# First bias on TensorE, Gelu from PSUM and a joined residual in the quantised feed-forward stage of a two-layer decoder

## The chip, the cores and the metric

One core of one Trainium2 chip runs the whole program. The metric is the device time of one execution in microseconds (us).

## The reference

The program is two decoder layers on x of shape 8 x 256 x 512; each layer has attention, cross attention and a feed-forward part, each followed by a residual and a layer norm. The change lies in the last part, the quantised feed-forward network of the second layer:

```python
def activation_quant(x):
    scale = 127.0 / jnp.clip(jnp.max(jnp.abs(x), axis=-1, keepdims=True), EPS_Q)
    return jnp.clip(jnp.round(x * scale), -128, 127) / scale
def weight_quant(w):
    return jnp.sign(w) * jnp.mean(jnp.abs(w))
def bit_linear(x, w, b, dim_in):
    x_norm = simple_rms_norm(x, dim_in)
    x_q = activation_quant(x_norm)
    w_q = weight_quant(w)
    return jnp.einsum('bsd,od->bso', x_q, w_q) + b
h = bit_linear(x, w1, b1, DIM)          # 512 -> 2048
h = jax.nn.gelu(h, approximate=False)
return bit_linear(h, w2, b2, INNER)     # 2048 -> 512
x = _layernorm(x + ffn(x), axis=-1)
```

## The kernel before

The kernel is written engine by engine: each stage is one block with a program for each of the five engines, which meet only through semaphores. An engine runs its program strictly in the order written; whatever waits holds up all that stands behind it. The last stage is `quantised_ffn_stage`. x lies in SBUF as 16 tiles of 128 rows and 512 columns, two tiles (q = 0, 1) to each of the 8 blocks b. Whole numbers up to 127 and signs are held in bfloat16 and multiplied exactly; one scale per row turns the product back ("unit").

Before the rounds the stage loads the weights (`raw`, four pieces of 2 MB) and the biases, ScalarE squares all rows of x (L2255) and takes the signs of the weights (L2213), and VectorE sums their magnitudes (L2315) and works out the scales of x (L2297 to L2309, with three Newton steps of `inverse_root`, L50).

A block then passes through these steps:
- VectorE scales x (L2328), GpSimd bounds and rounds it (L2277, L2280), TensorE transposes it (L2127) and ScalarE copies it out of PSUM (L2206).
- First product: eight chunks of 512 columns, four bfloat16 matmuls each (L2143), into four PSUM banks. VectorE reads each chunk, multiplies by the unit, adds the first bias and writes it to SBUF (L2340); ScalarE takes the Gelu in place (L2222).
- VectorE takes the greatest value (L2352) while ScalarE squares and sums the rows (L2233); some seventeen small VectorE steps give the scales; VectorE scales h (L2356), ScalarE subtracts the rounding constant (L2248), VectorE clamps (L2375).
- TensorE transposes h in 32 pieces (L2127), ScalarE copies them out in four parts (L2203), and the second product takes 2 x 16 matmuls (L2159).
- VectorE multiplies by the unit and adds the second bias (L2363), adds the residual (L2368), and normalises the rows (L85 to L101) into x.

The rounds overlap two blocks: in `round_of(b)`, b from 0 to 8, "here" is block b up to its clamped rows, "prev" is the transposes, second product and layer norm of block b-1, and "next" the preparation of x for b+1. `has` (L152) leaves out what isn't there at the ends. Rounds 1 to 6 are a loop on each engine whose waits count up in registers; rounds 0, 7 and 8 are written out. PSUM for transposes has two banks, used in turn (`Turns`, L127); a transpose waits for the copy two turns back. `Steps` (L26) lets an engine wait for its own last small step.

## Time and profile before

| what | value |
|---|---|
| median of 3 runs | 2926.22 us (2924.99 to 2927.89) |
| the profiled execution | 2924.51 us |
| its span | 2922.7 us |
| busy share of the span | TensorE 85%, VectorE 62%, ScalarE 43%, GpSimd 10% |
| mean granted TensorE clock | 0.948 of full |
| last stage | from about 2630 us to the end |

Times are in us from the start of the span, PE is TensorE, PEld its weight loads, DVE VectorE, ACT ScalarE, POOL GpSimd. In a timeline, rows of one kind that follow each other are merged: "x16" is the number of instructions, and the bracket at the end is the idle time ahead of the first and what ended it. A line number is that of the kernel before. A granted clock of 1.0 is 2.4 GHz, of 0.5 1.2 GHz. In a chain of waits each piece is what the next one waited for, or the work ahead of it on its engine.

### The profile page before, as it was taken

Reading aid. Unit: us, or ns where it says so; the run is one execution under the profiler, and the core shown is the slowest. Engines: PE = TensorE matmul, PEld = TensorE weight load, DVE = VectorE, ACT = ScalarE, POOL = GpSimd, SP = SyncE. Lnnn points to the kernel's source line nnn. Section 1 sums busy time; section 2 is a strip of 40 time slices with the busy share of each in tenths; the row PEclk is TensorE's granted clock in tenths of the full one; section 3 lists DMA queues with packets and bytes.
Section 4 is the critical chain, followed back from the end, with each engine's and each line's share of the span. In section 5 each row is a group of like instructions: output and inputs, shape, how many; then the busy total and the mean of one; then the engine's idle time right before and its main releaser. Section 6 shows DMA issues by size and latency. Waiting matters only on the chain. (4 is left out here: it accounts for less than half of the span.)

```text
span 2922.7 us, 46388 instructions
## 1 busy us (share of the span) xinstructions
PE 2475.3 (85%) x15730; PEld 1911.1 (65%) x15746; DVE 1802.4 (62%) x5199; ACT 1264.8 (43%) x2994; POOL 297.9 (10%) x535
## 2 busy tenths in 40 slices
PE   5889999999983999799999999995888888874664
PEld 3668999999863999476677766763655555541332
DVE  5656767667775566445445544454666666657886
ACT  2334545444433222244444444452544444436563
POOL 3211001000000000000000000002111111102220
PEclk8999999999996999999999999997999999996887
DMA  4101211212005000000000000001000000003001
GB/s 155 59 24 36 77 33 37 69 39 75 30 1 217 0 0 0 2 1 0 0 1 0 0 1 0 0 1 51 5 4 4 4 4 4 4 1 133 0 0 58
DMA packets 41151, 82.45 MB, mean 28 GB/s; under 512 B 4528, under 2 KB 17840, under 8 KB 39856
## 3 DMA queue, kind: packets, MB, share of 16 engines
q1 hardware_dynamic: 41008, 80.70, 7.8%
q8 instruction: 70, 1.15, 0.2%
q14 instruction: 73, 0.60, 0.1%
HBM read 72.30 MB, written 8.39 MB: 28 GB/s over the span
## 5 line engine op out<-in xcount | busy, mean ns | idle before, releaser
L1990 DVE TENSOR_REDUCE s_nmax<-s_a_ps 128x2 f32<-128x512 f32 x256 | 174.2, 686 | 195.1 <-PE s_a_ps L1772 188.1
L647 ACT ACTIVATE s_p<-s_ms,s_nmax 128x256 f32<-128x256 f32 x256 | 128.5, 503 | 194.4 <-DVE s_nmax L755 194.4
L755 DVE CUSTOM_DVE_ANT_0 s_ms<-s_s_ps,s_bias 128x256 f32<-128x256 f32 x256 | 98.1, 421 | 179.5 <-PE s_s_ps L525 179.0
L1375 ACT ACTIVATE l_wo_w<-l_wo_w,s_nmax 128x128 f32<-128x128 f32 (+1 forms) x256 | 114.4, 447 | 199.2 <-DVE s_nmax L1471 198.4
L508 PE MATMUL s_q_ps<-s_xT,s_wh 128*128 128x256 f32 x1024 | 189.9, 286 | 0.0
L1215 PE MATMUL s_s_ps<-l_wqb_w,s_lT 128*128 128x512 f32 x384 | 175.9, 597 | 16.5 <-DVE l_wo_w L1441 15.8
L914 PE MATMUL s_h_ps<-s_xh,s_t 128*128 128x256 f32 x704 | 173.3, 285 | 9.4 <-DVE s_xl L1002 9.4
L1886 ACT ACTIVATE s_pT<-s_s_ps 128x512 f32<-128x512 f32 x256 | 151.6, 606 | 59.7 <-PE s_s_ps L1785 57.6
L558 PE MATMUL s_y_ps<-s_wh,s_oT 128*128 128x512 f32 x512 | 175.6, 404 | 0.0
L914 PE MATMUL s_h_ps<-s_xl,s_t 128*128 128x256 f32 x704 | 172.7, 284 | 0.0
L508 PEld LDWEIGHTS s_q_ps<-s_xT,s_wh 128*128 128x128 f32 x1024 | 165.7, 194 | 6.0 <-issue 0.5
L1772 PE MATMUL s_a_ps<-s_kTz,s_qTx 128*128 128x256 f32 x512 | 137.2, 351 | 33.3 <-DVE s_nmax L1990 31.8
L1471 DVE CUSTOM_DVE_ANT_0 l_wo_w<-s_s_ps,s_bias 128x128 f32<-128x128 f32 (+1 forms) x256 | 80.9, 354 | 115.8 <-PE s_s_ps L1256 113.5
L508 PE MATMUL s_q_ps<-s_xT,s_wl 128*128 128x256 f32 x512 | 145.9, 285 | 0.0
L914 PEld LDWEIGHTS s_h_ps<-s_xh,s_t 128*128 128x128 f32 x704 | 135.2, 192 | 14.9 <-issue 11.2
L1772 PEld LDWEIGHTS s_a_ps<-s_kTz,s_qTx 128*128 128x128 f32 x512 | 83.7, 193 | 88.9 <-issue 44.8
L914 PEld LDWEIGHTS s_h_ps<-s_xl,s_t 128*128 128x128 f32 x704 | 135.2, 192 | 2.5
L642 ACT CAST s_qT<-s_q_ps 128x512 fp32r<-128x512 f32 x64 | 37.7, 589 | 213.0 <-PE s_q_ps L508 213.0
L1215 PEld LDWEIGHTS s_s_ps<-l_wqb_w,s_lT 128*128 128x128 f32 x384 | 71.0, 190 | 90.0 <-issue 65.1
L1456 DVE COPY l_wo_w<-s_s_ps 128x128 f32<-128x128 f32 x64 | 18.7, 292 | 179.1 <-PE s_s_ps L1215 175.5
L525 PE MATMUL s_s_ps<-s_kT,s_qT 128*128 128x256 f32 x768 | 117.2, 289 | 14.0 <-DVE s_qT L760 13.4
L965 ACT ACTIVATE s_u<-s_h_ps,s_scale 128x256 f32<-128x256 f32 x88 | 41.9, 477 | 200.1 <-PE s_h_ps L914 197.7
(304 smaller groups left out, 6713.2 us busy)
## 6 DMA issues: line engine op xcount, KB each, us to landing
s_x_raw<-kept SPq DMA_DIRECT2D x24, 512.0 KB, 3.3
s_c_in<-in_ctx_T SPq DMA_DIRECT2D x32, 256.0 KB, 2.8
l_wqb_w<-in_l_xwq SPq DMA_DIRECT2D x4, 1024.0 KB, 7.5
l_wqb_w<-in_l_xwo SPq DMA_DIRECT2D x4, 1024.0 KB, 10.0
kept<-s_x_raw SPq DMA_DIRECT2D x8, 512.0 KB, 2.7
l_wo_w<-in_l_wo SPq DMA_DIRECT2D x1, 4096.0 KB, 14.8
s_raw<-in_l_w1T SPq DMA_DIRECT2D x2, 2048.0 KB, 10.1
s_raw<-in_l_w2T SPq DMA_DIRECT2D x2, 2048.0 KB, 21.8
```

The costliest lines, as they stand in the source:

```text
L508: mm = pe.matmul(q_ps[:, j % 2 * S:(j % 2 + 1) * S], weight(of, "q", k, slice(j * HD, (j + 1) * HD)), xT[:, u % 2, by, k, :], start=(k == ...
L525: mm = pe.matmul(s_ps[:, h % 2, q * S:(q + 1) * S], qT[:, of, h % 4, q * P:(q + 1) * P], kT[:, u % 2, by, h % PER // 2, :], start=(n == 0) ...
L558: mm = pe.matmul(y_ps[:, q, :], oT[:, of, h % 4, q * P:(q + 1) * P], weight(by, "o", j, slice(0, D)), start=(j == 0 and n == 0), stop=(j = ...
L647: act.activation(p[:, h % PR, q, :], ms[:, h % 2, q, :], ACT.Exp, scale=-1.0, bias=nmax[:, h % PR, q:q + 1], accum_out=den[:, h % PR, q:q ...
L755: dve.tensor_tensor_reduce(ms[:, h % 2, q, :], s_ps[:, h % 2, q * S:(q + 1) * S], bias[:, h // PER % B, :], -SCALE, 3.0e38, ALU.add, ALU.m ...
L914: mm = pe.matmul(h_ps[:, f % 2, n * S:(n + 1) * S], t[:, k, f * P:(f + 1) * P], xp[:, k, :], start=(k == 0 and xp is xh), stop=(k == DK - ...
L1215: mm = pe.matmul(t, lT[:, k, q * P:(q + 1) * P], wqb_sb[:, k, chunk * 512:(chunk + 1) * 512], start=(k == 0), stop=(k == QL - 1))
L1375: act.activation(p[:, h % PR, q, 0:(q + 1) * P], ms[:, h % 2, q, 0:(q + 1) * P], ACT.Exp, scale=-1.0, bias=nmax[:, h % PR, q:q + 1], accum ...
L1471: last = dve.tensor_tensor_reduce(ms[:, h % 2, q, 0:n], s_ps[:, at[1], q * S:q * S + n], bias[:, S - n:S], -SCALE, 3.0e38, ALU.add, ALU.mi ...
L1772: mm = pe.matmul(a_ps[:, n % 2, q * S:(q + 1) * S], qTx[:, g % 2, pair, q * P:(q + 1) * P], kTz[:, GH * g + 2 * pair + e, :], start=True, ...
L1886: act.activation(pT[:, j % GH, :, :], s_ps[:, j % 2, :].rearrange("p (k n) -> p k n", k=QT), ACT.Exp).then_inc(s_out, 1)
L1990: dve.tensor_reduce(nmax[:, g % 2, :, 2 * pair + e], a_ps[:, n % 2, :].rearrange("p (q k) -> p q k", q=QT), AX_X, ALU.max, negate=True).th ...
```

## The change

- The first bias goes to TensorE. Each chunk of the first product gets a fifth matmul (L2152 of the changed kernel) of float32r operands: `b1_hl` holds the bias on each partition as its high part, on partitions 64 to 95 as its low part; `per_unit` holds, for each of the 16 row tiles, the inverse of the unit at partitions 32 apart (high part, low part, high part), transposed. Their product is bias over unit, which the later multiplication by the unit turns to the bias.
- New work ahead of the rounds makes these: `bias_rows` on VectorE, one cast on ScalarE (L2276), one transpose on TensorE (L2199), one memset on GpSimd.
- VectorE's bias step is gone. ScalarE's Gelu (L2233) reads the chunk in PSUM, with the unit as its scale, and frees the bank.
- h has two buffers, used by even and odd blocks. The second and `hw` lie where the first weights were loaded (`raw[1]`, `raw[0]`), and b1 is loaded into the first tile of h.
- GpSimd adds the second bias to x, a block at a time (`x_biased`, L2301), after x was quantised; L2399 then multiplies and adds that sum in one step, and the adding of the residual is gone.
- ScalarE's roundings of h (L2254) move from the end of round b to round b+1, behind its Gelus and Squares. TensorE does both halves of a first product, then the transposes of h. VectorE normalises the rows of b-1 ahead of the clamps of b.
- Two small steps of the scales are folded into others, and the unit of h has two buffers.
- All rounds are written out, none loops.
- In the opening stage two semaphores become one.

```diff
@@ first stage
-            first = Steps(dve, first_steps, FIRST_STEPS)
+            first = Steps(dve, norm_steps, FIRST_STEPS)
@@ tiles of the last stage
-        b1_sb = m.sb("b1", [P, INNER])
+        b1_hl = m.sb("b1_hl", [P, INNER], F32R)
+        unit_hl = m.sb("unit_hl", [P, P])
+        select = m.sb("select", [P, T])
+        per_unit = m.sb("per_unit", [P, T, P], F32R)
-        h = m.sb("h", [P, QT, INNER])
-        hw = m.sb("hw", [P, QT, INNER])
+        h_own = m.sb("h", [P, QT, INNER])
+        h = [h_own[:, :, :], raw[1][:, :].rearrange("p (q n) -> p q n", q=QT)]
+        hw = raw[0][:, :].rearrange("p (q n) -> p q n", q=QT)
+        b1_sb = h_own[:, 0, :]
@@ TensorE
-                        mm = pe.matmul(v_ps[:, c, :], xqT[:, q, k, :], sg1[:, k, c * 512:(c + 1) * 512],
-                                       start=(k == 0), stop=(k == DK - 1))
-                    mm.then_inc(v_full, 1)
+                        pe.matmul(v_ps[:, c, :], xqT[:, q, k, :], sg1[:, k, c * 512:(c + 1) * 512],
+                                  start=(k == 0), stop=False)
+                    if b == 0 and q == 0 and c == 0:
+                        pe.wait_ge(u_steps, 6)
+                    pe.matmul(v_ps[:, c, :], per_unit[:, b * QT + q, :], b1_hl[:, c * 512:(c + 1) * 512],
+                              start=False, stop=True).then_inc(v_full, 1)
@@ ScalarE, round_of
-                        act.wait_ge(v_out, b * H_USES + 4 + n + 1)
-                        ge = act.activation(h[:, q, c * 512:(c + 1) * 512], h[:, q, c * 512:(c + 1) * 512], ACT.Gelu)
+                        act.wait_ge(v_full, b * H_USES + n + 1)
+                        ge = act.activation(h[b % 2][:, q, c * 512:(c + 1) * 512], v_ps[:, n % IC, :], ACT.Gelu,
+                                            scale=xs["unit"][:, b * QT + q:b * QT + q + 1])
+                        ge.then_inc(v_out, 1)
+                if has(b, "prev"):
+                    for q in range(QT):
+                        act.wait_ge(hw_full, (b - 1) * QT + q + 1)
+                        act.activation(hq[:, q, :], hw[:, q, :], ACT.Identity, bias=round_off[:, :]).then_inc(rounded, 1)
-                if has(b, "here"):
-                    for q in range(QT):
-
-                        act.wait_ge(hw_full, b * QT + q + 1)
-                        act.activation(hq[:, q, :], hw[:, q, :], ACT.Identity, bias=round_off[:, :]).then_inc(rounded, 1)
@@ GpSimd
+            for b in range(B):
+                x_biased(b)
+                if b + 1 < B:
+                    x_bounded(b + 1)
@@ VectorE, bias_rows
+                dve.tensor_tensor(b1_hl[64:96, :], b1_sb[64:96, :], b1_hl[64:96, :].bitcast(F32), ALU.subtract).then_inc(u_steps, 1)
+                dve.tensor_tensor(per_unit[:, :, :], y_ps[:, 1, 0:P].unsqueeze(1).broadcast_to([P, T, P]),
+                                  select[:, :].unsqueeze(2).broadcast_to([P, T, P]), ALU.mult).then_inc(u_steps, 1)
@@ VectorE, round_of
-                        dve.scalar_tensor_tensor(out=h[:, q, c], in0=v_ps[:, n % IC, :],
-                                                 scalar=xs["unit"][:, bass.ds(b * QT + q, 1)], in1=b1_sb[:, c],
-                                                 op0=ALU.mult, op1=ALU.add).then_inc(v_out, 1)
-                        ad = dve.tensor_tensor(r[:, q, :], r[:, q, :], core.x[:, (b - 1) * QT + q, :], ALU.add)
+                        dve.scalar_tensor_tensor(out=r[:, q, :], in0=y_ps[:, q, :], scalar=h_unit[:, (b - 1) % 2, q:q + 1],
+                                                 in1=core.x[:, (b - 1) * QT + q, :], op0=ALU.mult, op1=ALU.add).then_inc(y_out, 1)
```

ScalarE's program for round 7 before (s_h is h, s_a_ps the transposes in PSUM, s_hqT their copies):

```order
L2222 ACTIVATE s_h<-s_h 128x512 x4
L2203 COPY s_hqT<-s_a_ps 128x1024 x2
L2222 ACTIVATE s_h<-s_h 128x512 x4
L2233 ACTIVATE s_sq,s_h_squares<-s_h 128x2048 x2
L2203 COPY s_hqT<-s_a_ps 128x1024 x2
L2248 ACTIVATE s_hq<-s_hw,s_round_off 128x2048 x2
L2203 COPY s_hqT<-s_a_ps 128x1024 x4
```
And in the changed kernel, from the start of round 6 to its copies of x, and on through round 7's (s_raw is odd blocks' h at L2233 and L2241, and `hw` at L2254):

```order
L2233 ACTIVATE s_h<-s_v_ps,s_x_unit 128x512 x8
L2241 ACTIVATE s_sq,s_h_squares<-s_h 128x2048 x2
L2254 ACTIVATE s_hq<-s_raw,s_round_off 128x2048 x2
L2212 COPY s_hqT<-s_a_ps 128x1024 x4
L2215 COPY s_xqT<-s_a_ps 128x512 x2
L2233 ACTIVATE s_raw<-s_v_ps,s_x_unit 128x512 x8
L2241 ACTIVATE s_sq,s_h_squares<-s_raw 128x2048 x2
L2254 ACTIVATE s_hq<-s_raw,s_round_off 128x2048 x2
L2212 COPY s_hqT<-s_a_ps 128x1024 x4
```
The roundings moved from behind the second pair of copies, at the end of the round of their own block, to between the Squares and the copies of the next block's round; before, half of the copies stood between the Gelus.

TensorE's program for rounds 7 and 8 before (s_v_ps takes the first product, s_y_ps the second):

```order
L2143 MATMUL s_v_ps<-s_sg,s_xqT 128x512 x16
L2127 MATMUL s_a_ps<-identb,s_hq 128x128 x16
L2143 MATMUL s_v_ps<-s_sg,s_xqT 128x512 x16
L2127 MATMUL s_a_ps<-identb,s_hq 128x128 x16
L2159 MATMUL s_y_ps<-s_sg,s_hqT 128x512 x32
L2127 MATMUL s_a_ps<-identb,s_hq 128x128 x32
L2159 MATMUL s_y_ps<-s_sg,s_hqT 128x512 x32
```
And the end of round 7 and round 8 in the changed kernel:

```order
L2152 MATMUL s_v_ps<-s_b_hl,s_per_unit 128x512
L2148 MATMUL s_v_ps<-s_sg,s_xqT 128x512 x4
L2152 MATMUL s_v_ps<-s_b_hl,s_per_unit 128x512
L2132 MATMUL s_a_ps<-identb,s_hq 128x128 x32
L2167 MATMUL s_y_ps<-s_sg,s_hqT 128x512 x32
L2132 MATMUL s_a_ps<-identb,s_hq 128x128 x32
L2167 MATMUL s_y_ps<-s_sg,s_hqT 128x512 x32
```
The transposes of h no longer stand between the halves of the first product; all eight chunks, each with its fifth matmul, come ahead of them.

VectorE's program of round 7 before, from the scaling of h on (s_hw is the scaled h, s_hq the rounded one, s_r the rows to be normalised):

```order
L2356 TENSOR_SCALAR s_hw<-s_h,s_h_levels 128x2048 x2
L2309 TENSOR_SCALAR s_h_unit<-s_h_most,s_scale 128x2
L2363 SCALAR_TENSOR_TENSOR s_r<-s_y_ps,s_unit_last,s_b 128x512 x2
L2368 TENSOR_TENSOR s_r<-s_r,x 128x512 x2
L85 BN_STATS s_bn<-s_r 128x6 x2
L89 BN_AGGR s_mv<-s_bn 128x2 x2
L2375 TENSOR_SCALAR s_hq<-s_hq 128x2048 x2
L95 TENSOR_SCALAR s_var<-s_mv 128x2
```
And the seam of rounds 5 and 6 in the changed kernel, from the last Newton steps of the layer norm on:

```order
L55 TENSOR_TENSOR s_nt<-s_nt,s_var 128x2
L56 SCALAR_TENSOR_TENSOR s_rstd<-s_nt,s_rstd 128x2
L101 TENSOR_SCALAR x<-s_r,s_mv,s_rstd 128x512 x2
L2410 TENSOR_SCALAR s_hq<-s_hq 128x2048 x2
L2350 TENSOR_SCALAR s_xw<-x,s_x_levels 128x512 x2
L2383 TENSOR_REDUCE s_h_most<-s_h 128x2
```
The clamps L2410 now stand behind the whole layer norm of the block before, and the next block's greatest value L2383 right behind the clamps, where the bias steps were.

## Rows read from the trace of the kernel before

**Rows 1.** Timeline of VectorE, last stage: start us, us, engine, line, operation
```profile
2656.54 0.23 DVE L2309 TENSOR_SCALAR s_x_unit<-s_x_most,s_scale 128x16 f32<-128x16 f32 x1
...
2700.68 4.41 DVE L2352 TENSOR_REDUCE s_h_most<-s_h 128x2 f32<-128x4096 f32 x1
...
2874.76 4.42 DVE L2352 TENSOR_REDUCE s_h_most<-s_h 128x2 f32<-128x4096 f32 x1 [0.70 <-ACT s_h L2222]
...
2908.32 1.00 DVE L101 TENSOR_SCALAR x<-s_r,s_mv,s_rstd 128x512 f32<-128x512 f32 x2
```
**Rows 2.** Busy us of PE, PEld, DVE, ACT, POOL; PEclk, DMA, in one round
```profile
2721.65:2750.47 28.82, 19.77 (x102) 9.20 (x104) 25.13 (x55) 17.32 (x20) 6.90 (x4) 0.86 0.00 0
```
**Rows 3.** The chain of waits in the same round: start us, us, what
```profile
2722.46 5.26 PE s_v_ps L2143 x16
...
2735.31 5.31 PE s_y_ps L2159 x16
...
2741.96 3.80 ACT s_hq L2248 x2
```
**Rows 4.** Groups by form, last stage: busy us, mean ns, idle before and releasers
```profile
L2340 DVE SCALAR_TENSOR_TENSOR s_h<-s_v_ps,s_x_unit,s_b 128x512 f32<-128x512 f32 x64 | 46.1, 748 | 18.1 <-PE s_v_ps L2143 14.1 <-DVE s_unit_last L2335 1.6
L2222 ACT ACTIVATE s_h<-s_h 128x512 f32<-128x512 f32 x64 | 39.3, 631 | 46.9 <-DVE s_h L2340 46.0
...
L2368 DVE TENSOR_TENSOR s_r<-s_r,x 128x512 f32<-128x512 f32 x16 | 10.3, 685 | 0.0
...
L2304 DVE TENSOR_SCALAR s_h_levels<-s_h_levels 128x2 f32<-128x2 f32 x8 | 1.4, 170 | 0.3
```
**Rows 5.** Timeline of TensorE, stages before (twelve L558 matmuls in the first two)
```profile
406.65 0.39 PE L558 MATMUL s_y_ps<-s_wh,s_oT 128*128 128x512 f32 x1
...
409.22 0.40 PE L558 MATMUL s_y_ps<-s_wh,s_oT 128*128 128x512 f32 x1
...
2614.84 3.70 PE L1753 MATMUL s_f_ps<-s_wo,s_oT 128*128 128x512 f32 x8 [2.34 <-DVE s_oT L2007]
```
**Rows 6.** Timeline of TensorE, last stage
```profile
2680.23 3.59 PE L2143 MATMUL s_v_ps<-s_sg,s_xqT 128*128 128x512 bf16 x8 [1.76 <-ACT s_xqT L2206]
...
2722.46 5.25 PE L2143 MATMUL s_v_ps<-s_sg,s_xqT 128*128 128x512 bf16 x16 [4.45 <-DVE s_h L2340]
...
2740.46 0.61 PE L2127 MATMUL s_a_ps<-identb,s_xq 128*128 128x128 bf16 x8
2742.09 3.62 PE L2143 MATMUL s_v_ps<-s_sg,s_xqT 128*128 128x512 bf16 x15 [1.02 <-ACT s_xqT L2206]
...
2890.36 1.89 PE L2127 MATMUL s_a_ps<-identb,s_hq 128*128 128x128 bf16 x16 [5.92 <-DVE s_hq L2375]
...
2894.67 7.73 PE L2159 MATMUL s_y_ps<-s_sg,s_hqT 128*128 128x512 bf16 x31 [0.22 <-ACT s_hqT L2203]
```
**Rows 7.** Groups by form, stages before: ScalarE, GpSimd, weight loads
```profile
L965 ACT ACTIVATE s_u<-s_h_ps,s_scale 128x256 f32<-128x256 f32 x88 | 41.9, 477 | 200.1 <-PE s_h_ps L914 197.7 <-DVE s_g L1023 2.4
...
L385 POOL TENSOR_TENSOR x<-x,s_bo 128x1024 f32<-128x1024 f32 x8 | 19.0, 2374 | 52.1 <-PE s_a_ps L442 42.6 <-DMA s_bo<-in_l_bo 9.5
...
L558 PEld LDWEIGHTS s_y_ps<-s_wh,s_oT 128*128 128x128 f32 x512 | 99.3, 194 | 22.0 <-DVE s_oT L777 0.3
```
**Rows 8.** Timeline of ScalarE, last stage
```profile
2656.80 1.07 ACT L2206 COPY s_xqT<-s_a_ps 128x512 bf16<-128x512 bf16 x2 [7.65 <-PE s_a_ps L2127]
...
2672.02 7.12 ACT L2213 ACTIVATE s_sg<-s_raw 128x4096 bf16<-128x4096 f32 x2
...
2729.19 1.91 ACT L2233 ACTIVATE s_sq<-s_h 128x2048 bf16<-128x2048 f32 x1
...
2733.04 0.18 ACT L2233 ACTIVATION_READ_ACCUMULATOR s_sq<-s_h 128x1 f32 x1
2733.33 1.93 ACT L2203 COPY s_hqT<-s_a_ps 128x1024 bf16<-128x1024 bf16 x2
...
2741.85 3.90 ACT L2248 ACTIVATE s_hq<-s_hw,s_round_off 128x2048 bf16<-128x2048 f32 x2
```

More of the change, by code:

```diff
@@ L717, in normalise @@
                     if turn < B:
-                        first.round(turn)
+                        first.round(turn, 1)
                         row_statistics(core, first, dve, xb, w)
@@ L721, in normalise @@
                     else:
-                        norm.round(turn - B, 1)
+                        norm.round(turn - B, 1 + B * FIRST_STEPS)
                         row_statistics(core, norm, dve, xb, w)
@@ L2165, in round_of @@
                     pe.wait_ge(a_out, x_over(b, QT - 1) + 3)
-                for q in range(QT):
-                    if has(b, "here"):
+                if has(b, "here"):
+                    for q in range(QT):
                         first_product(b, q)
-                    if has(b, "prev"):
+                if b == 0:
+                    magnitude(1)
+                if has(b, "prev"):
+                    for q in range(QT):
                         gelus_over(b, q)
-                if isinstance(b, int) and b == 0:
-                    magnitude(1)
                 if has(b, "prev"):
@@ L2216, in round_of @@
             def round_of(b):
-                late = [("prev", "h", q, half) for q in range(QT) for half in range(2)] if has(b, "prev") else []
                 if has(b, "here"):
@@ L2243, in round_of @@
                         rows_over(a_turns.at(b, use), a_turns.bank(b, use), *use[1:])
-                if has(b, "here"):
-                    for q in range(QT):
-                        act.wait_ge(hw_full, b * QT + q + 1)
-                        act.activation(hq[:, q, :], hw[:, q, :], ACT.Identity, bias=round_off[:, :]).then_inc(rounded, 1)
             act.sem_inc(a_out, 2)
+            act.sem_inc(v_out, 4)
             act.wait_ge(fixed, 1)
@@ L2259, in _ @@
                 rows_over(q, q % 2, "x", q, 0)
-            round_of(0)
-            with act.Fori(1, B - 1) as b:
+            act.wait_ge(b1_full, 16)
+            act.copy(b1_hl[:, :], b1_sb).then_inc(b1_hi, 1)
+            act.wait_ge(xs_steps, SCALE_STEPS + 2)
+            act.wait_ge(u_steps, 5)
+            for b in range(B + 1):
                 round_of(b)
-            round_of(B - 1)
-            round_of(B)
         @block.gpsimd
```

155 lines of the change are left out of this document (81 added, 74 removed).

## The prediction

> **What bounds the kernel now.** Only the last stage changes, so I read it alone. The end first: the last VectorE work, L101, starts at 2908.32 and takes 1.00, so the stage's arithmetic ends at 2909.32 [rows 1]. The greatest value of each block (L2352) is taken at 2700.68 in round 1 and at 2874.76 in round 7, six rounds later, 29.01 us each [rows 1]; from there to the end it is 34.56 us. Then the busy time by engine: in one loop round of 28.82 us VectorE works 25.13, TensorE 19.77, ScalarE 17.32, GpSimd 6.90, and TensorE's granted clock is 0.86 of full [rows 2]. VectorE looks like the bound, and the chain of waits agrees only in part: in one round it goes through the first product (2722.46), the Gelu and Square behind it, the second product (2735.31) and the roundings L2248 (2741.96) [rows 3], and only then back to VectorE's clamp, layer norm and the next bias steps. So a round is one long chain through three engines, with VectorE's queue as its closing link. What matters is how long the new order makes that chain, not what is taken from VectorE's busy time.
>
> **What is removed.** VectorE loses eight L2340 per round (748 ns each, 0.72 from start to start), two L2368 (685), and the copy L2335 and two more small steps of L2304's size, 0.2 from start to start [rows 4]: 5.8 + 1.3 + 0.6 = 7.7 us of 25.1. These shorten the path only where VectorE is still waited for.
>
> **What is added on TensorE.** One float32r matmul of 512 columns behind every four of bfloat16, 64 in all. The opening stage shows that form: twelve starts from 406.65 to 409.22, eleven steps, 0.234 us each [rows 5]. A bfloat16 one takes (3.62-0.17)/16 = 0.216 at full clock (one record is missing there, 16 run) and (3.59-0.17)/8 = 0.427 at half, with 0.17 for the drain [rows 6]. A chunk, four plus one, then takes 1.10 us at full clock, 2.13 at half; a round's eight take 8.8. Bounds for the float32r pass from these rows: 0.216, as bfloat16, and 0.42, if its weight load of 0.194 [rows 7] stands bare each time. I take 0.234, because the row is the very form.
> The nearest warning is the plain float32 tile, L1753: eight in 3.70, (3.70-0.17)/8 = 0.44 for 512 columns [rows 5]. The Trainium skill, page "FP8 and Floating Point Precision", section "TensorE Precision Notes", says that true FP32 takes four passes through the array, which would be 0.86 here; L1753 at 0.44 doesn't bear out four, and L558 with operands cast to fp32r shows one. By the page's figure the sum would grow by 64 x 0.63 = 40 us.
>
> **Gelu from PSUM.** An ACTIVATE that reads 256 columns of PSUM with a scale per partition takes 477 ns; L2222 takes 631 for 512 from SBUF [rows 4, 7]. By ScalarE's 0.83 ns per column (a Square of 2048 takes 1.91 [rows 8], (1910-631)/1536) that is 477 + 213 = 690. The Gelus come one per chunk of 1.10, so only the last lies on the path. Bounds 0.63 and 0.72: 0.1 us a round.
>
> **GpSimd's join** of residual and second bias is L385's form, 128x1024, 2374 ns [rows 7]. GpSimd is busy 6.9 us of a round, so 9.3 now, and the sum is wanted a round later: nothing on the path. Without that cover it would cost at most 2.4 a round. The unrolling and the shared semaphore of the opening stage I cost at nothing but the loop's gaps, which the next count leaves out.
>
> **The new round.** The order on ScalarE decides it. Rounding and transposed copies of block b-1 used to stand at the end of round b-1, beside VectorE's layer norm; now they stand behind eight Gelus and two Squares of block b. TensorE does all first products, then waits for the clamped rows. Where one thing waits for the next:
> - eight chunks 8.8, drain and last Gelu 0.9, two Squares at 2.03 each (2729.19 to 2733.22) 4.05 [rows 8];
> - two roundings 3.9 [rows 8], with the first clamp under the second one;
> - two copies at 0.93 (1.93 for two, L2203 [rows 8]), then eight transposes, 0.6: 2.6 to the second product;
> - 32 matmuls: 6.9 at full clock; after 5.92 us of idle and the transposes the last round took 7.73 [rows 6]. TensorE will idle 7.8 us each round (0.9 + 4.05 + 1.9 + 0.9), so I take 7.7;
> - transposes of x and their first copies: from 2740.46 to 2742.09 [rows 6], 1.6.
> Sum 8.8 + 0.9 + 4.05 + 3.9 + 2.6 + 7.7 + 1.6 = 29.6 us against 29.01. VectorE has clamps 1.3, x 0.9, reduction 4.4, fifteen small steps 2.9, scaling 2.5, unit 0.2, layer norm 6.3: 18.5, hence 11 idle, waiting for the roundings with the next reduction queued behind them. Six rounds: **+3.5 us**.
>
> **The start.** Before, the unit of x (L2309) was ready at 2656.77 [rows 1]. Now: two steps fewer, 2656.4; seven small steps, 2657.8; ScalarE's cast of the bias, 2048 columns, 2.0 like a rounding, behind its copies of x (2656.80, 1.07) ends at 2659.5 [rows 8]; then come two VectorE passes over 2048 elements, for which L2352 with 4096 in 4.41 [rows 1] gives 2.2, taken as 2.3: 2664.1. The first chunk's float32r pass waits for it and TensorE has idled some 4 us, so 0.43 + 2 x 2.13 + 5 x 1.10 = 10.2: 2674.3. Last Gelu 2675.2, Squares 2679.3, two signs 7.12 [rows 8] 2686.4, copies of x 1.07, and round 1 begins at 2687.5 (before: 2680.23 [rows 6]). Its first product, TensorE cold again, takes 2 x 2.13 + 6 x 1.10 = 10.9; then 0.9, 4.05, 3.9 to 2707.3; clamp 0.7, x 0.9: reduction at 2708.9 instead of 2700.68, **+8.2**.
>
> **The end.** From the last roundings: clamp 0.75, then reduction 4.45, small steps 2.95, scaling and unit 2.75, layer norm 6.3, clamp 0.7, then 4.4 to the second product (2890.36 to 2894.67) and from there 14.65 less one L2368 pair, 13.35 [rows 6, 1]. After the reduction's start that is 34.9 against 34.56, and no x rounding of 0.9 stands ahead of it: **-0.5**.
> Sum: 8.2 + 3.5 - 0.5 = **+11.2 us**. The profiled execution took 2924.51 (span 2922.7), so 2935.7 for it; the median of the runs shown is 1.7 higher, 2926.22, and gets 2937.4, say **2937**.
>
> **Rivals.**
> (a) VectorE was the bound and is relieved. Then the round falls to the next busiest engine, TensorE at 19.77 + 8 x 0.234, some 21.6 us: 6 x -7.4 = -44, with +8.2 for the start about 2890. For it: 25.13 busy of 28.82. Against: VectorE is released by ScalarE's roundings, and these follow the Gelus in program order; it decides only if rounding b-1 could pass Squares b. 5%.
> (b) The clock stays at 2.4 GHz: second products 6.9 in all seven rounds, -5.6, and with a float32r pass at 0.216 -1.2 more: +4.4 to +5.6, about 2931, no change. Against: behind an idle of 4.45 us sixteen first products took 5.25 instead of 3.62 [rows 6], and the new gap is longer. 17%.
> (c) The float32r weight load isn't hidden behind a bfloat16 matmul: 64 x 0.19 = +12 on top, 2949. For it: the load takes 194 ns [rows 7], nearly a whole bfloat16 matmul of 216. Against: in the opening stage it was hidden. The Trainium skill, page "TensorE: Matmul & The Clock Gate", section "LDWEIGHTS (loading the stationary operand)", gives 107 ns for 128 columns whatever the type, by which (c) could not be; the rows with 194 contradict that. 11%.
> (d) The pass runs like plain float32: 64 x 0.21 = +13 at L1753's price, 2951. 3%. By the four passes of the page "FP8 and Floating Point Precision" of the Trainium skill it would be 2977.
> My forecast has 64%.
>
> **Numbers.** A measurement of this kernel tells 0.2%, 5.9 us, from no change: faster is below 2920.4, slower above 2932.1. Faster: (a) and a little, 0.06. Same: (b) and the low edge of the forecast, 0.20. Slower: the rest of it, (c), (d), 0.74. The range takes in (b) with bfloat16's price, the forecast and (c): 2927 to 2950.
>
> **What would show it.** Right: reductions of h 29 to 30 us apart in rounds 1 to 7; VectorE waiting some 10 us a round for the rounding; TensorE idle 7 to 8 us before the transposes of h and at half clock behind it; round 1's reduction near 2709. Wrong: rounds of 22 us with ScalarE or TensorE nearly full (a); chunks of 1.3 us or more (c, d); granted clock above 0.95 in the rounds (b).

## The result and the profile after

| | before | changed |
|---|---|---|
| median | 2926.22 us (9 runs, 2920.71 to 2928.8) | 2935.08 us (9 runs, 2933.4 to 2940.42) |
| ratio | | 1.0039, 95% interval 1.003 to 1.0048 |
| profiled execution, span | 2924.51, 2922.7 | 2935.08, 2933.2 |
| mean granted TensorE clock | 0.948 | 0.947 |

The change makes the kernel slower by 0.39%, 8.9 us of the medians. The timeline of VectorE in the last stage of the changed kernel, rows answering to [rows 1]; L2383 is the reduction over h, once L2352:
```profile
2656.85 0.23 DVE L2331 TENSOR_SCALAR s_x_unit<-s_x_most,s_scale 128x16 f32<-128x16 f32 x1
...
2709.28 4.41 DVE L2383 TENSOR_REDUCE s_h_most<-s_raw 128x2 f32<-128x4096 f32 x1
...
2885.77 4.41 DVE L2383 TENSOR_REDUCE s_h_most<-s_raw 128x2 f32<-128x4096 f32 x1
...
2918.88 1.00 DVE L101 TENSOR_SCALAR x<-s_r,s_mv,s_rstd 128x512 f32<-128x512 f32 x2
```
Round 1's reduction comes 8.60 us later than before, round 7's (2885.77) 11.01, and the last work 10.56. Of this 0.71 lies ahead of the stage, whose first weight transfer is issued at 2629.96 in the kernel before and at 2630.67 here. So the start of the stage lost 7.9 us, six rounds lost 2.4 (29.41 each instead of 29.01), and the end gained 0.45: 9.85 in the stage.

Busy time in one round, answering to [rows 2] (PE, PEld, DVE, ACT, POOL, granted clock, DMA share, GB/s):
```profile
2739.40:2768.14 28.74, 19.66 (x113) 10.46 (x113) 19.51 (x43) 18.32 (x21) 9.22 (x6) 0.86 0.00 0
```
VectorE's 25.13 us have become 19.51, and the round, 28.74, is hardly shorter than the 28.82 of [rows 2] (on average it is longer): no engine is busy for more than 20 us of it. Where the time goes is seen in the same round on TensorE:
```profile
2740.68 6.85 PE L2167 MATMUL s_y_ps<-s_sg,s_hqT 128*128 128x512 bf16 x31
...
2748.93 1.04 PE L2148 MATMUL s_v_ps<-s_sg,s_xqT 128*128 128x512 bf16 x4 [0.94 <-ACT s_xqT L2215]
2749.61 0.58 PE L2152 MATMUL s_v_ps<-s_b_hl,s_per_unit 128*128 128x512 f32 x1
...
2756.72 1.04 PE L2148 MATMUL s_v_ps<-s_sg,s_xqT 128*128 128x512 bf16 x4
...
2765.67 1.89 PE L2132 MATMUL s_a_ps<-identb,s_hq 128*128 128x128 bf16 x16 [7.68 <-DVE s_hq L2410]
...
2769.98 0.63 PE L2167 MATMUL s_y_ps<-s_sg,s_hqT 128*128 128x512 bf16 x1 [0.22 <-ACT s_hqT L2212]
```
on ScalarE:
```profile
2758.03 0.69 ACT L2233 ACTIVATE s_raw<-s_v_ps,s_x_unit 128x512 f32<-128x512 f32 x1 [0.43 <-PE s_v_ps L2152]
2758.75 1.91 ACT L2241 ACTIVATE s_sq<-s_raw 128x2048 bf16<-128x2048 f32 x1
...
2762.81 3.89 ACT L2254 ACTIVATE s_hq<-s_raw,s_round_off 128x2048 bf16<-128x2048 f32 x2
2766.74 1.93 ACT L2212 COPY s_hqT<-s_a_ps 128x1024 bf16<-128x1024 bf16 x2
```
and on VectorE:
```profile
2746.99 1.99 DVE L2326 SCALAR_TENSOR_TENSOR s_h_levels<-s_h_levels,s_h_root 128x2 f32<-128x2 f32 x1
...
2764.92 0.69 DVE L2410 TENSOR_SCALAR s_hq<-s_hq 128x2048 bf16<-128x2048 bf16 x1 [6.92 <-ACT s_hq L2254]
```
Follow the starts: eight chunks from 2748.93, the last Gelu at 2758.03, Squares at 2758.75, roundings at 2762.81, VectorE's clamp at 2764.92 after waiting 6.92 us, and TensorE, which waited 7.68 us for it, at 2765.67, at half clock (the granted clock is 0.50 from 2764 to 2770 and 1.00 from 2771 on; 16 transposes take 1.89 us, 1.06 at full). Each step waits for the one before it.

The new operations by form (of L2233 the row of the even blocks):
```profile
L2152 PE MATMUL s_v_ps<-s_b_hl,s_per_unit 128*128 128x512 f32 x64 | 38.8, 606 | 4.5 <-DVE s_per_unit L2370 4.5
...
L2233 ACT ACTIVATE s_h<-s_v_ps,s_x_unit 128x512 f32<-128x512 f32 x32 | 22.0, 687 | 16.1 <-PE s_v_ps L2152 15.9
...
L2301 POOL TENSOR_TENSOR x<-x,s_b 128x1024 f32<-128x1024 f32 x8 | 18.9, 2362 | 3.7 <-DMA s_b<-in_l_b 3.7
...
L2152 PEld LDWEIGHTS s_v_ps<-s_b_hl,s_per_unit 128*128 128x128 f32 x64 | 12.7, 198 | 13.3 <-DVE s_per_unit L2370 5.4 <-issue 0.8
```
The start, ScalarE's cast, VectorE's two long passes for the bias, and TensorE behind them and at the beginning of round 1:
```profile
2658.07 1.91 ACT L2276 CAST s_b_hl<-s_h 128x2048 fp32r<-128x2048 f32 x1
...
2660.01 2.47 DVE L2367 TENSOR_TENSOR s_b_hl<-s_h,s_b_hl 32x2048 fp32r<-32x2048 f32 x1 [1.90 <-ACT s_b_hl L2276]
2662.51 2.29 DVE L2370 TENSOR_TENSOR s_per_unit<-s_y_ps,s_select 128x2048 fp32r<-128x2048 f32 x1
...
2664.86 0.79 PE L2152 MATMUL s_v_ps<-s_b_hl,s_per_unit 128*128 128x512 f32 x1 [4.50 <-DVE s_per_unit L2370]
...
2688.41 1.49 PE L2148 MATMUL s_v_ps<-s_sg,s_xqT 128*128 128x512 bf16 x3 [12.98 <-ACT s_xqT L2215]
```

### The profile page after: what moved, and what is told of

Its sections match the earlier page's. It is cut to its first block and busy times, and to the rows that moved or that the text cites. A ratio compares the mean times of both kernels' runs of the same rounds, so it can differ in the third digit from the quotient of the medians.

```text
span 2933.2 us, 45897 instructions
## 1 busy us (share of the span) xinstructions
PE 2481.7 (85%) x15795; PEld 1923.9 (66%) x15811; DVE 1759.9 (60%) x5102; ACT 1273.8 (43%) x2995; POOL 316.2 (11%) x544
## 5 line engine op out<-in xcount | busy, mean ns | idle before, releaser
L558 PE MATMUL s_y_ps<-s_wh,s_oT 128*128 128x512 f32 x512 | 175.5, 404 | 0.0
L914 PEld LDWEIGHTS s_h_ps<-s_xh,s_t 128*128 128x128 f32 x704 | 135.4, 192 | 14.9 <-issue 11.2
L1215 PEld LDWEIGHTS s_s_ps<-l_wqb_w,s_lT 128*128 128x128 f32 x384 | 71.0, 190 | 90.0 <-issue 65.1
```

What stands on the lines that cost most here:

```text
L558: mm = pe.matmul(y_ps[:, q, :], oT[:, of, h % 4, q * P:(q + 1) * P], weight(by, "o", j, slice(0, D)), start=(j == 0 and n == 0), stop=(j = ...
L914: mm = pe.matmul(h_ps[:, f % 2, n * S:(n + 1) * S], t[:, k, f * P:(f + 1) * P], xp[:, k, :], start=(k == 0 and xp is xh), stop=(k == DK - ...
L1215: mm = pe.matmul(t, lT[:, k, q * P:(q + 1) * P], wqb_sb[:, k, chunk * 512:(chunk + 1) * 512], start=(k == 0), stop=(k == QL - 1))
```

## The experiments

Profiled executions of different kernels enter the last stage up to 10 us apart, though nothing ahead of it differs (its first weight transfer is issued at 2625.45 to 2635.14), so beside the median the table has the stage in the trace: from that issue to the start of the last L101. "Ratio" is to the kernel before, whose median in these comparisons was 2924.8 to 2925.1. The number in brackets is that of the experiment.

| kernel | median us | ratio, 95% interval | stage us |
|---|---|---|---|
| before | 2926.2 | | 278.4 |
| changed | 2935.1 | 1.003 to 1.0048 | 288.2 |
| changed, old order (1) | 2883.8 | 0.984 to 0.9873 | 237.8 |
| changed, without float32r pass (2) | 2917.9 | 0.9968 to 0.9988 | 270.4 |
| before, unrolled only (3) | 2920.5 | 0.9978 to 0.9997 | 272.5 |
| before, unrolled, new order (4) | 2976.2 | 1.0156 to 1.019 | 328.5 |
| changed, without GpSimd's addition (5) | 2936.1 | 1.0024 to 1.0049 | 288.2 |
| changed, gap filled with matmuls (6) | 2930.5 | 1.0008 to 1.0027 | 284.3 |
| changed, roundings put back, TensorE's order kept (7) | 2882.6 | 0.9833 to 0.9866 | 237.7 |
| old order, without GpSimd's addition (8) | 2886.7 | 0.9851 to 0.9884 | 237.7 |
| old order, addition moved (9) | 2885.5 | 0.9849 to 0.9881 | 237.0 |
| as 9, early transposes (10) | 2881.3 | 0.9841 to 0.9873 | 233.3 |
| as 10, clamps first (11) | 2874.1 | 0.9814 to 0.9847 | 226.9 |
| as 11, signs early (12) | 2868.8 | 0.9792 to 0.9824 | 220.5 |

**1. The old order under the new arithmetic.** ScalarE's part of the edit (TensorE's and VectorE's follow the kernel before):
```diff
@@ scalar, round_of: behind Gelu n == 3, copies of h^T; behind the Squares, the other two
+                        if n == IC - 1 and late:
+                            for use in late[:2]:
+                                rows_over(...)
-                if has(b, "prev"):
-                    for q in range(QT):
-                        act.wait_ge(hw_full, (b - 1) * QT + q + 1)
-                        act.activation(hq[:, q, :], hw[:, q, :], ACT.Identity, ...)
@@ at the end of round_of
+                if has(b, "here"):
+                    for q in range(QT):
+                        act.wait_ge(hw_full, b * QT + q + 1)
+                        act.activation(hq[:, q, :], hw[:, q, :], ACT.Identity, ...)
```


> The changed kernel with the order of the kernel before put back: the roundings of block b at the end of round b on ScalarE, the copies of h^T between the Gelus and behind the Squares, each half's transposes behind its first product on TensorE, the clamps ahead of the layer norm's scales on VectorE. The float32r pass, the Gelu from PSUM, GpSimd's join, the two h buffers and the start stay. Theory (the new order of the roundings made the long chain of 29.4 us a round): rounds of 21 to 24 us, the greatest values of h 21 to 24 us apart, whole kernel 2880 to 2900 us. Rival one (the loss is the pass, the start and the slower clock): rounds of 28 us or more, 2925 to 2935 us. Rival two (VectorE's queue makes the round, with GpSimd's long join in its way): rounds of 25 us, 2905 to 2915.


Measured 2883.77 us, 51 less than the changed kernel and 41 less than before: the theory's range, and both rivals out. VectorE's timeline of two rounds, in which L2381 is the reduction:
```profile
2726.43 4.42 DVE L2381 TENSOR_REDUCE s_h_most<-s_h 128x2 f32<-128x4096 f32 x1 [2.24 <-ACT s_h L2233]
...
2749.11 4.42 DVE L2381 TENSOR_REDUCE s_h_most<-s_raw 128x2 f32<-128x4096 f32 x1 [1.72 <-ACT s_raw L2233]
...
2754.56 2.32 DVE L54 SCALAR_TENSOR_TENSOR s_h_tmp<-s_h_root 128x2 f32<-128x2 f32 x1
...
2771.52 4.42 DVE L2381 TENSOR_REDUCE s_h_most<-s_h 128x2 f32<-128x4096 f32 x1 [1.73 <-ACT s_h L2233]
```
A round is 21.8 to 23.5 us (22.6 on average, from 2704.66 to 2840.13 in six), and VectorE waits 1.7 to 2.3 us of it for the Gelus, where in the changed kernel it waited 8.1 to 9.5 for the roundings. The arithmetic that the change moved off VectorE pays, once the roundings stand in their own round.

**2. The float32r pass alone.** The four bfloat16 matmuls end the chunk, so the first bias is left out (shortened; the wait for its preparation stays, ahead of the very first chunk's last matmul):
```diff
-                    pe.matmul(v_ps[:, c, :], per_unit[:, b * QT + q, :], b1_hl[:, c * 512:(c + 1) * 512],
-                              start=False, stop=True).then_inc(v_full, 1)
+                    mm.then_inc(v_full, 1)
```


> The changed kernel without the 64 float32r matmuls (so the first bias is left out of the sum; its preparation and the wait for it are kept). Theory (the pass costs its 0.234 us each at full clock and all eight of a round lie on the chain): 1.9 us less in each of eight rounds, 15 to 17 us less than the changed kernel, 2918 to 2920 us. Rival, a weight load that is not hidden (0.42 each): 27 us less, 2908. Rival, the pass lies beside other work: no change, 2935.


Measured 2917.86 us, 17.2 less (the stage 17.8 less), 0.27 us for each of 64, just outside the expected 15 to 17. The eight chunks of a round are now one row:
```profile
2742.24 7.08 PE L2150 MATMUL s_v_ps<-s_sg,s_xqT 128*128 128x512 bf16 x32 [0.94 <-ACT s_xqT L2214]
```
(7.08 - 0.17)/8 is 0.864 a chunk, against 1.113 with the pass (seven steps from 2748.93 to 2756.72 above), so a pass is 0.25 at full clock, 2.0 us a round. Six rounds are 27.08 us each instead of 29.41, 2.3 less, so some 0.3 of it isn't the passes themselves. The pass lies on the path as supposed, and it's far from the 27 us of a load that isn't hidden.

**3. The unrolling alone.** On each engine, with fixed indices in place of the counted ones:
```diff
-            with dve.Fori(1, B - 1) as b:
+            for b in range(1, B + 1):
                 round_of(b)
-            round_of(B - 1)
-            round_of(B)
```


> The kernel before with its loops written out and nothing else changed. Theory: the loop costs VectorE and the others about 0.4 to 1 us a round, part of it beside other work: 2 to 6 us less, 2920 to 2924 us. Rival (the loop is free): 2926.


Measured 2920.53 us, 4.3 less (the stage 5.8 less), and the six rounds are 28.35 us each instead of 29.01. The interval ends at 0.9997, so that it is faster is shown, its size less well.

**4. The new order alone, on the kernel before.**
```diff
@@ scalar, round_of, behind the Squares of block b
+                if has(b, "prev"):
+                    for q in range(QT):
+                        act.wait_ge(hw_full, (b - 1) * QT + q + 1)
+                        act.activation(hq[:, q, :], hw[:, q, :], ACT.Identity, ...)
@@ vector, behind the bias steps of block b
+                if has(b, "prev"):
+                    for q in range(QT):
+                        dve.wait_ge(rounded, (b - 1) * QT + q + 1)
+                        dve.tensor_scalar(hq[:, q, :], hq[:, q, :], 127.0, -128.0, ...)
```


> The kernel before, unrolled, with the new order alone: roundings and transposed copies of block b-1 behind the Gelus and Squares of block b on ScalarE, all first products ahead of all transposes of h on TensorE, clamps of block b-1 behind the bias steps of block b on VectorE. Bias still on VectorE, Gelu from SBUF, one h buffer. Theory (the order alone makes the round one chain): residual and layer norm 7.6 us, eight bias steps 5.8, Gelu 0.7, Squares 4.05, roundings 3.9, copies and transposes 2.6, second product 7.7, about 32 us a round in place of 29, so 15 to 25 us more than the kernel before, 2940 to 2950 us. Rival (the order is harmless, the loss is in the pass and the start): 2920 to 2926.


Measured 2976.22 us, 55.7 more than the unrolled kernel and 51.4 more than the kernel before, for which 15 to 25 were expected: the theory's sign, at more than twice its size. One round, busy times as above, and pieces of its chain of waits (start, us, what):
```profile
2783.00:2819.43 36.43, 21.98 (x107) 10.71 (x106) 25.23 (x56) 17.82 (x21) 6.92 (x5) 0.73 0.00 0
```
```profile
2783.09 4.34 DVE s_h_most L2348
...
2802.54 6.03 PE s_v_ps L2143 x16
...
2810.04 2.01 ACT s_sq L2228 x2
...
2814.10 3.90 ACT s_hq L2236 x2
...
2819.51 4.34 DVE s_h_most L2348
```
The expected chain ran over the second product. The real one runs over VectorE's own queue: reduction 4.3, scales and scaling 6.5, residual and layer norm 7.6, bias steps tied to TensorE's first product (a granted clock of 0.60 from 2802.50 to 2808.60), Squares, roundings, clamp, and again the reduction; 36 us. With the bias still on VectorE, nearly its whole queue stands in the chain, 25.23 us of busy time, and the waits come on top.

**5. GpSimd's addition left out of the changed kernel.**
```diff
-                pool.tensor_tensor(xb, xb, b2_sb[...].unsqueeze(1).broadcast_to([P, QT, D]), ALU.add).then_inc(xb_full, 1)
+                pool.sem_inc(xb_full, 1)
```


> The changed kernel without GpSimd's addition of the second bias (the second bias is left out of the output). Theory (in the changed kernel the 128x1024 addition only delays one small VectorE step by 1.8 us, and VectorE waits 7 to 8 us for the roundings behind it): the small step back from 1.99 to 0.16 us, the time the same within 1.5 us, 2933.5 to 2935.5. Rival (the delay is on the path): 1.8 us less in each of six rounds, 2924.


Measured 2936.09 us (2932.11 to 2937.85), 1.0 above the changed kernel and 0.6 above the expected range, no difference that these runs tell; the stage is 288.2 as in the changed kernel. The small step is back at its length:
```profile
2749.66 0.16 DVE L2326 SCALAR_TENSOR_TENSOR s_h_levels<-s_h_levels,s_h_root 128x2 f32<-128x2 f32 x1
```
and in this same round VectorE then waits 8.76 us for the rounding instead of 6.92, 1.84 more: the stall only ate slack.

**6. The gap filled.** TensorE multiplies for nothing while it would wait:
```diff
+                if has(b, "here") and has(b, "prev"):
+                    pe.wait_ge(y_out, b * QT)
+                    for n in range(32):
+                        pe.matmul(y_ps[:, 1, :], xqT[:, 1, n % DK, :], sg1[:, n % DK, 0:512], start=True, stop=True)
```


> The changed kernel with 32 more bfloat16 matmuls of 512 columns in each of rounds 1 to 7, in the 7.7 us in which TensorE waits for the clamped rows; they write a bank of y_ps that the second product overwrites later, and nothing reads them. Theory (the clock falls in that gap, and half speed costs 0.4 us of the second product, and some more of the transposes and of the first product in each round): granted clock of the kernel up from 0.947, second products 6.9 us instead of 6.85 to 7.78, 3 to 7 us less than the changed kernel, 2928 to 2932. Rival (the extra matmuls, 32 x 0.216 = 6.9 us, run longer than the gap or the clock falls all the same): no gain or a loss, 2935 or more.


Measured 2930.47 us, 4.6 less. The windows of a round show the clock at full:
```profile
2767.36:2795.92 28.56, 25.63 (x148) 12.42 (x145) 19.52 (x43) 18.10 (x21) 9.23 (x6) 1.00 0.00 1
```
The six rounds are 28.68 us on average instead of 29.41. So the idling costs 0.73 us a round through the clock. It is a price of the chain, not its cause.

**7. The roundings put back, TensorE's order kept.** As 1, but TensorE keeps the new order, and ScalarE makes the first copies behind the last Gelu:
```diff
@@ tensor, round_of, against 1
-                for q in range(QT):
-                    if has(b, "here"):
-                        first_product(b, q)
-                    if has(b, "prev"):
-                        gelus_over(b, q)
+                if has(b, "here"):
+                    for q in range(QT):
+                        first_product(b, q)
+                if has(b, "prev"):
+                    for q in range(QT):
+                        gelus_over(b, q)
@@ scalar, against 1
-                        if n == IC - 1 and late:
+                        if n == 2 * IC - 1 and late:
```


> The changed kernel with the roundings alone put back: ScalarE rounds block b at the end of round b and makes the transposed copies of h behind the last Gelu (the first half) and behind the Squares (the second), VectorE clamps ahead of the layer norm's scales; TensorE keeps the new order, all first products ahead of all transposes of h. Theory (what costs the 50 us is that the roundings stand behind the Gelus and Squares of the next block, not TensorE's order): within 6 us of the kernel with the old order, 2880 to 2890 us. Rival (TensorE's order is half of it): 2900 to 2915.


Measured 2882.6 us, within 1.2 of the whole old order. Two of VectorE's reductions, one round apart:
```profile
2747.53 4.42 DVE L2382 TENSOR_REDUCE s_h_most<-s_raw 128x2 f32<-128x4096 f32 x1 [0.51 <-ACT s_raw L2234]
...
2770.10 4.42 DVE L2382 TENSOR_REDUCE s_h_most<-s_h 128x2 f32<-128x4096 f32 x1 [0.47 <-ACT s_h L2234]
```
A round is 22.57 us, 22.58 in 1. TensorE's order, which looks like the change's main rearrangement, is worth nothing that these runs tell; ScalarE's order (the roundings in their own round, behind the copies of h^T), and VectorE's clamps with it, is worth all of the 50 us. Roundings, copies and clamps were moved together, so their shares are not known one by one.

**8, 9. GpSimd's addition in the old order: left out, and moved.** Left out with the edit of 5; the move:
```diff
 def x_bounded(b):
+                        if q == 0:
+                            pool.wait_ge(xw_full, b * QT + QT)
+                            x_biased(b - 1)
@@ at the end
-                x_biased(b)
-                if b + 1 < B:
-                    x_bounded(b + 1)
+            x_biased(B - 1)
```


> The changed kernel with the old order (2883.8 us, rounds of 22.4 to 23.5 us, VectorE busy for 20.7 of them) without GpSimd's addition of the second bias (left out of the output). Theory (VectorE is close to the bound there, and each addition stops one of its small steps for 2.1 us): 1 to 2.1 us less in each of seven rounds, 2870 to 2877 us. Rival (TensorE and ScalarE make the round): within 2 us of 2883.8.

> The changed kernel with the old order, and GpSimd's addition moved ahead of the bounding of the next block's x, behind both of its roundings, where it runs beside VectorE's wait for the Gelus and its reduction over h. Nothing is left out. Theory (an addition of GpSimd doesn't stop a reduction of VectorE: at 2703.71 to 2706.07 in the kernel with the old order the reduction from 2704.66 took 4.42 us as ever): the same gain as without the addition, 2870 to 2877 us. Rival (it stops any instruction of VectorE, here the reduction): 2883. Rival (TensorE and ScalarE make the round): within 2 us of 2883.8.


Measured 2886.67 and 2885.49 us: no gain. The theory of both is out; the last rival's 2 us around 2883.8 take in the second, and the first lies 2.9 above. VectorE's stall of 2.1 us is gone, and it waits 2.2 us for the Gelus. TensorE's timeline of the second half of the second product, with the addition (experiment 1), and without:
```profile
2755.16 3.63 PE L2167 MATMUL s_y_ps<-s_sg,s_hqT 128*128 128x512 bf16 x16 [2.45 <-ACT s_hqT L2211]
```
```profile
2754.57 5.31 PE L2167 MATMUL s_y_ps<-s_sg,s_hqT 128*128 128x512 bf16 x16 [2.44 <-ACT s_hqT L2211]
```
In both it waits 2.4 us for ScalarE's copies of h^T, which stand behind the Squares, and then it runs at full clock in one and at half in the other, 1.7 us longer. The clock decides how long a round is (the two granted clocks are 1.00 and 0.93 over the whole round). With the addition, rounds 2 to 7 are 22.4 to 22.7 us where this half runs at full clock (one is 21.8) and 23.46 in the one where it runs at half. Without it, or with it moved, they are 21.8 at full clock (one 22.85) and again 23.46 at half, but at half in three rounds of six. So without the stall the round is 0.6 to 0.9 us shorter at full clock, and the rounds at half clock give it back: 22.6 on average either way in 8, 22.8 in 9. Why the clock falls in more of them isn't shown; what it falls behind is TensorE's wait of 2.4 us for ScalarE's copies.

**10. Early transposes.** The second half's transposes between that half's second and third chunk, its copies behind the sixth Gelu:
```diff
 def first_product(b, q):
                 for c in range(IC):
+                    if q == 1 and c == 2 and has(b, "prev"):
+                        gelus_over(b, 1)
@@ scalar
-                        if n == IC - 1 and late:
+                        if n in (IC - 1, IC + 1) and late:
```


> The kernel with the addition under the reduction, and on top TensorE's transposes of the second half of h between the second and the third chunk of that half's first product, with ScalarE's copies of them behind the sixth Gelu in place of behind the Squares. Theory (TensorE waits 2.45 us in each round for those copies and the clock falls with it): 0.5 to 1.5 us less in each of seven rounds than the kernel with the addition under the reduction, 2860 to 2872 us. Rival (the Squares, now later by 1.9 us, make VectorE's scales late): no gain or a loss of up to 10 us, 2872 to 2885.


Measured 2881.3 us (2875.02 to 2885.64); the interval of the ratio overlaps with that of 9, so by the runs the gain is open, and the expected 2860 to 2872 were missed; the rival's range holds it, but not by the rival's means, since the rounds did get shorter. The stage in the trace is 3.7 us shorter. Rounds are 21.5 us, with the clock at full, but the last one with an addition beside it is 25.06. There GpSimd adds for block 7 while VectorE works out the scales:
```profile
2810.75 2.35 POOL L2303 TENSOR_TENSOR x<-x,s_b 128x1024 f32<-128x1024 f32 x1
...
2811.13 1.99 DVE L2327 SCALAR_TENSOR_TENSOR s_h_levels<-s_h_levels,s_h_root 128x2 f32<-128x2 f32 x1
2813.16 2.48 DVE L2391 TENSOR_SCALAR s_raw<-s_h,s_h_levels 128x2048 f32<-128x2048 f32 x2
...
2814.48 3.90 ACT L2262 ACTIVATE s_hq<-s_raw,s_round_off 128x2048 bf16<-128x2048 f32 x2 [2.62 <-DVE s_raw L2391]
```
```profile
2782.04:2803.54 21.50, 18.54 (x114) 9.37 (x113) 17.68 (x43) 17.52 (x21) 9.21 (x6) 1.00 0.00 1
2803.54:2828.60 25.06, 20.27 (x114) 10.19 (x113) 18.63 (x40) 17.73 (x21) 9.11 (x5) 0.93 0.00 0
```
The windows are the round before and this one. In the round before, without an addition there, the small step takes 0.16. Here the same stall, 1.8 us, lies on the path: ScalarE waits 2.62 us for the scaled rows instead of 0.79, and the clock falls to 0.93 behind it.

**11. Clamps first, the addition behind them.** (`x_biased` inside `x_bounded`, from 9, goes too.)
```diff
@@ vector: row_statistics moved from ahead of the clamps to behind them
@@ gpsimd
-            for b in range(1, B):
-                x_bounded(b)
-            x_biased(B - 1)
+            for b in range(B):
+                if b + 1 < B:
+                    x_bounded(b + 1)
+                pool.wait_ge(hq_full, b * QT + QT)
+                x_biased(b)
```


> The kernel with early transposes, with two more moves: VectorE clamps h ahead of the layer norm's statistics instead of behind them, and GpSimd's addition comes behind these clamps (beside the statistics) instead of ahead of the bounding of the next x. Nothing is left out. In the kernel with early transposes each round of 21.5 us has TensorE waiting 1.37 us for the clamps, 0.91 for GpSimd's x and 0.68 for ScalarE's copies of x. Theory (these waits are the round, since each engine is busy for 17 to 18.5 us): 1 to 2 us less in each of six rounds, 19.5 to 20.5 us a round, 2868 to 2876 us. Rival (VectorE, now stopped for 2.3 us by the addition among its small steps, becomes the bound): rounds of 21 us or more, 2878 to 2885.


Measured 2874.1 us, inside the range, but by other means than expected: the rounds are 21.24 us, hardly shorter. Of 6.4 us in the stage 3.8 are the last round of 10 (25.06, now 21.30), where the addition no longer stands in the way, 1.7 lie behind the last reduction (30.18, now 28.45), and the five other rounds give 0.26 each or less. The rounds of 19.5 to 20.5 us were not reached. What bounds the round is seen on ScalarE and VectorE:
```profile
2741.52 4.42 DVE L2384 TENSOR_REDUCE s_h_most<-s_raw 128x2 f32<-128x4096 f32 x1 [1.18 <-ACT s_raw L2235]
...
2749.23 2.48 DVE L2391 TENSOR_SCALAR s_raw<-s_raw,s_h_levels 128x2048 f32<-128x2048 f32 x2
...
2762.76 4.42 DVE L2384 TENSOR_REDUCE s_h_most<-s_h 128x2 f32<-128x4096 f32 x1 [1.18 <-ACT s_h L2235]
```
```profile
2750.55 3.90 ACT L2262 ACTIVATE s_hq<-s_raw,s_round_off 128x2048 bf16<-128x2048 f32 x2 [1.97 <-DVE s_raw L2391]
2754.36 2.40 ACT L2235 ACTIVATE s_h<-s_v_ps,s_x_unit 128x512 f32<-128x512 f32 x4
...
2759.59 1.97 ACT L2213 COPY s_hqT<-s_a_ps 128x1024 bf16<-128x1024 bf16 x2
```
Reduction 4.42, small steps to 2749.23, the first scaling to 2750.55, two roundings to 2754.36, then eight Gelus and four copies to 2762.76, where the next reduction waits for them. A loop of two engines, 21.24 us, in which TensorE's waits lie beside the path.

**12. The signs early.**
```diff
             signs(0)
             signs(1)
-            for q in range(QT):
-                rows_over(q, q % 2, "x", q, 0)
             act.wait_ge(b1_full, 16)
             act.copy(b1_hl[:, :], b1_sb).then_inc(b1_hi, 1)
+            signs(2)
+            for q in range(QT):
+                rows_over(q, q % 2, "x", q, 0)
+            signs(3)
@@ round_of
-                if b == 0:
-                    signs(2)
-                    signs(3)
```


> The kernel with the clamps first, with a different start: ScalarE casts the bias and takes the signs of the first half of w2 in its 7.2 us of waiting ahead of the copies of x, and those of the second half behind them, where it waits 5.6 to 5.8 us for the first chunk; before, both halves stood ahead of round 1 (7.12 us). Nothing is left out. Theory (the start is a chain through ScalarE, which waits in it twice): the bias's cast off the way, 1.9 us, and round 1 earlier by 3 to 4 us on top, 4 to 7 us less than the kernel with the clamps first, 2867 to 2870 us. Rival (w2 lands too late, and the signs hold up the copies of x and all behind them): no gain or a loss, 2874 to 2880.


Measured 2868.83 us, 5.3 less than 11 (the stage 6.4 less; the intervals of the two ratios overlap a little), and 1.9% less than the kernel before (interval 1.76% to 2.08%). Round 1's reduction starts 65.1 us after the first weight transfer is issued (2629.53 to 2694.67) instead of 71.2, and the rounds are 21.23 us as before. It beats both kernels.

## Why the prediction held

**The sum.** Expected +8.2, +3.5 and -0.5, together +11.2 in the stage. Measured in the stage, with the 0.71 us ahead of it taken off: +7.89, +2.41 and -0.45, together +9.85. The good match of the last two is partly an accident of where the lines are drawn. The forecast's -0.5 holds 0.9 us for an x rounding that the last block lacks, and this stands ahead of round 7's reduction, so that in the rows it falls to the rounds. Like for like the rounds were forecast at +2.6 and measured at +2.4, and the end at +0.3 and measured at -0.45. The profiled executions differ by 10.57 us, and the medians by 8.9, so 2937 was 1.9 us too high: the changed kernel's profiled execution is its median run, while that of before lay 1.7 below its own.

**The start.** VectorE's second long pass (2662.51 and 2.29) ends at 2664.80, 0.71 off 2664.09, forecast 2664.1; round 1's reduction in the same way comes at 2708.57, forecast 2708.9.

**The round, term by term**, on average of rounds 1 to 6 where nothing else is said.
- Chunks, drain and last Gelu: 9.82 us from 2748.93 to the Squares at 2758.75, expected 9.7. A chunk takes 1.113 (1.10), the Gelu from PSUM 687 ns (690). The pass was mis-sized a little, 0.25 for 0.234.
- Squares: 4.06 (4.05).
- Roundings to the second product: 7.17 in four rounds of six and 6.6 in two, 6.99 on average, expected 3.9 + 2.6 = 6.5. The transposes run at half clock (1.89 for 16), which the term had left out.
- Second product: 7.7 in every round was too much. Its rows read 6.85 to 7.78, and from its start to the transposes of x it is 7.12, since the clock comes back before it or early in it. With x, 1.55 for 1.6, the terms add up to 29.54, and the forecast's, before rounding to 29.6, to 29.55. That they meet so closely is luck: two errors of about 0.5 us, both from the clock, nearly cancel. (The 29.41 between reductions is 0.13 less because round 7 has no x rounding.)
- The end's 0.8 us is the same mistake: from the last second product's start (2907.28) to the end of L101 (2919.88) it is 12.60, expected 13.35, and its row reads 6.89 where the forecast had carried over 7.73.
- TensorE's idle time: 7.68 for 7.8. VectorE's: expected 10 to 11 us, measured 29.4 less 19.5, 9.9, of which 8.1 to 9.5 are waits for the roundings and the rest the short gaps between its steps. Its work was taken as 18.5 us, and the 1 us more is less than the one stalled step, which the prediction hadn't seen.

**GpSimd's addition** was put down at nothing on the path, and that is so (experiment 5), but the cover was drawn wrongly. It isn't only GpSimd's time: the addition holds up one small step of VectorE for 1.8 us, and what hid that was VectorE's wait for the roundings. The price without cover was given as 2.4 a round at most; in experiment 10 the stall on the path is 1.8 and the round 3.6 longer.

**The unrolling** was put at nothing but the loop's gaps, which the sum left out. Alone it is worth 4.3 us. The forecast didn't suffer, most likely because the new round was built from its own chain and not from the old round's length, but as an account of the change the sentence was wrong: the old round to be beaten was 28.35 us without its loop.

**The order.** The prediction's central step, that ScalarE's order makes the chain, is shown by 7 and by 1; that the clamped rows are what TensorE waits for, too. But it told TensorE's new order as part of the same chain, and 7 shows that to cost nothing that the runs tell.

**The rivals.** (a) was turned down because rounding b-1 can't pass the Squares of b; with that undone the kernel takes 2883.8, near the 2890 worked out for (a). (b) would have given -5.6 to -6.8; holding the clock up gave -4.6 (6), but left alone it falls in every round: 16 transposes take 1.89 us behind each gap. (c) and (d) are out by 2: 17.2 us for 64 passes. On (c) the rows side with neither page nor fear: the load's records last 198 ns in the changed kernel too, for which the Trainium skill, page "TensorE: Matmul & The Clock Gate", section "LDWEIGHTS (loading the stationary operand)", has 107, and yet a chunk grows by 0.25 only, about what the pass's columns take.

**The account.** Unrolling -4.3; the moves off VectorE, with start and pass, -36.7 (2920.5 to 2883.8); the new order +51.3. What the change gained by its arithmetic and the unrolling, 41 us, it gave back in its order, and about 10 more (8.9 by the medians of the result; the kernel before ran at 2924.8 in the experiments and at 2926.2 there). On the unrolled kernel before the same order cost 55.7, so all that the change did besides (the two h buffers, the lighter VectorE) softens it by some 4 us at most.

What stays open: whether a round shorter than 21.2 us can be had by putting some of the next block's Gelus ahead of the roundings, which would open the loop of 11, wasn't tried.

## What to carry to other kernels

Before work is taken off the busiest engine, ask what releases it: here it was released by another engine's step in program order, and moving that step behind the next block's work cost 51 us, more than all the savings together. A shorter wait is not yet a shorter round either: in 8 and 9 what VectorE no longer lost went into rounds at half clock. Build the new round as one chain from measured rows and compare it with the old round's length; busy shares would have promised a gain. When a change mixes an order and an arithmetic, run them apart, since the good half may be worth keeping.
